# A gather ring of 72 slots instead of 64, its last eight in the memory of two buffers of the x pass, and expert units spread by another estimate of room

## The chip, the cores and the metric

One core of one Trainium2 chip. The metric is the device time of one execution in microseconds (us). Before the change three runs gave 2422.8, 2426.01 and 2431.03 us, so the median is 2426.01 us.

## The reference

The input is x (12500 nodes x 256), 200000 edges (src, dst, weight; sorted by dst) and the weights of two layers.

```python
x = x + gnn(layernorm(x))      # support = xn @ W (256x256); out[dst] += weight * support[src]; out + b
x = x + ffn(layernorm(x)[None])
# ffn: router on the mean over all nodes -> softmax over 8 experts, capacity scale, top 2, softmax of the 2
#      h = gelu(x @ W1[e] + b1[e]) (256 -> 512); y = h @ W2[e] + b2[e] (512 -> 256)
#      out = layer_norm(sum of 2 gated experts + x) * gamma + beta
```

dst is floor(12500 * u^2) with u uniform, so low nodes have many edges and high nodes few. Everything is float32.

## The kernel before

**Slots and tiles.** The edges, taken from the highest dst down, are cut into NE = 1564 slots of 128 edges. The nodes are 98 tiles of 128, numbered in the same order: tile 0 has about 5 slots, tiles 1 to 40 some 8 to 10, tile 72 about 16, tile 96 about 66 and tile 97, the last, about 158. For each slot GpSimd (POOL) issues one indirect DMA that gathers the 128 source rows into a slot of the ring G (L559). VectorE (DVE) builds a one-hot matrix with the edge weights (L1053), in a ring of 8. TensorE (PE) multiplies one by the other and accumulates in PSUM (L1374, two matmuls a slot).

**The ring.** G has RING = 64 slots. From slot 64 on, POOL waits at L552 until PE has done all slots up to three behind the one whose memory it takes (s_main at least s - 61). The first 96 slots (FRESH) gather from x itself, later ones from xr_d, a copy of x scaled by each row's 1/std. That copy is made in the x pass at the start: SyncE (SP) loads 25 groups of four tiles into XBUF = 18 buffers XS (L370), DVE takes the moments, ScalarE (ACT) scales (L773), SP stores to xr_d (L419). The groups are stored in lots of 4, 4, 4, 5, 4, 2 and 2. Groups 18 to 24 go into buffers 0 to 6 again. XS lies in the memory that the expert units use later.

**The sections.** Where PE has finished a tile's slots there is an END event: PE runs `chores` for the tiles before (transpose, product with W, transpose of the normalised row: L1321, L1325, L1326, L1330) and `begin` for the shared slots of the next tile (L1336, L1337), and ACT runs `section`, which copies PSUM to SBUF and normalises. For each group of four tiles ACT computes the roots together (`root`, L672 to L686), in the section of a tile whose number leaves 3 when divided by 4. The next section's L1330, in the tile whose number divides by 4, waits for the row XH that ACT can only make behind these roots (L692).

**The units.** All eight experts are computed ahead of the router for eight groups of tiles: 64 expert units. Up (L1346) and down (L1357) of a unit run between slots; ACT does the gelu (L753) and the copy out (L761). The first eight units have two tiles, the others four. `events()` places the units: from tile 14 on a tile has a `room`, 0.75 of its slots less 3.5, and the units are dealt out in proportion. A table of 168 due slots and kinds, EVT, goes to the chip, and PE, ACT and SP walk it in the same order. So a unit's place in the sequence of slots is fixed; only its time is not.

**PE's loop.** PE's slots run in a loop of 195 iterations of 8 slots and 4 more (L1409). The place in the ring is computed from registers at the head of each iteration: `(i & 7) * 2048`. Behind every second slot PE's sequencer compares the next due slot with its own (L1382), and where it is reached, `event` runs (L1383 and on).

**The second stage.** After slot 1563 come the router and the two chosen experts for the remaining 17 groups.

Of the kernel before, what the change touches and what calls it, by code (L numbers as in the profile page):

```python
# [4 lines left out]
P = 128  # L5
# [4 lines left out]
NE = (EDGES + 2 * P - 1) // (2 * P) * 2  # L10
FULL = EDGES // P
NC = (NE + P - 1) // P
RING, GS, OHR = 64, 16, 8
FRESH, XBUF = 96, 18
LOTS = (4, 4, 4, 5, 4, 2, 2)
SHIFT = (NT - 1) * P
LN_EPS = 1e-5
# [60 lines left out]
def events():  # L78
    share = lambda t: min(max(t, 0), NODES / P) / (NODES / P)
    slots = [NE * (share(NT - t) ** 0.5 - share(NT - 1 - t) ** 0.5) for t in range(NT)]  # L80
    most = [0.75 if t == NT - 1 else 1.0 for t in range(NT)]
    room = [max(0.0, 0.75 * slots[t] - 3.5) * most[t] if t >= 14 else 0.0 for t in range(NT)]
    size = [len(tiles(k // E)) / GT for k in range(UNITS)] + [1.0]
    free, u, out = 0.0, 0, []
    for t in range(NT):
        free += room[t] * sum(size) / sum(room)
        n = 0
        while u + n <= UNITS and (free >= size[u + n] / 2 or t == NT - 1):
            free -= size[u + n]
            n += 1  # L90
        kinds = [UPS if k == 0 else DOWNS if k == UNITS else BOTH for k in range(u, u + n)]
        mine = [(round(64 * most[t] * (k + 1) / (n + 1)) / 64, kind, u + k) for k, kind in enumerate(kinds)]
        if t == NT - 1:
            mine += [(k / 32, EXTRA, NT - 1 + k) for k in range(VIRTUAL)]
        out += [(t, *m) for m in sorted(mine)]
        if t < NT - 1:
            out.append((t, 1.0, END, t))
        u += n
    return out
# [7 lines left out]
def gnn_ffn(nc, x, dflat, srct, dstt, wt, W, b, Wr, br, W1, b1t, W2, b2, gamma, beta, cst, iota_e, evt, out):  # L107
# [13 lines left out]
    with ctx:  # L121
# [70 lines left out]
        YU = early("YU", [P, 2, GT * P])  # L192
        H = early("H", [P, 4, GT * P])
        YE = early("YE", [P, 2, GT * D])
        XS = At(w_at)("XS", [P, XBUF, GT, D])
        Gf = G[:, :, :].rearrange("p r d -> p (r d)")

        TABLES = 28
        first = At(g_at + 4 * TABLES * D)
# [2 lines left out]
        LOW = first("LOW", [P, NE], i32)  # L202
        IE, EV = first("IE", [NT, NE]), first("EV", [NT + 1, 2 * NEV])
        cmpb, cmpt = first("cmpb", [P, NC, NT], bf16), At(low_at)("cmpt", [NT, NE], bf16)
        assert first.at <= g_at + 4 * RING * D

        moments = At(yt_at)
        XST, XMV = moments("XST", [P, 2, GT, 6]), moments("XMV", [P, NT, 2])
# [152 lines left out]
        def _(e):  # L361
# [3 lines left out]
            def load_x(g):  # L365
                k = g % XBUF
                if g >= XBUF:
                    e.wait_ge(xs_st[lot_of[g - XBUF]], 16 * LOTS[lot_of[g - XBUF]])
                a, n = g * GT, len(xtiles(g)) - (g == XG - 1)
                e.dma_start(XS[:, k, 0:n, :].rearrange("p t d -> p (t d)"), x[a * P:(a + n) * P, :].rearrange("(p t) d -> p (t d)", p=P)).then_inc(xs_in[k], 16)  # L370
                if g == XG - 1:
                    e.dma_start(XS[0:LAST, k, n, :], x[(NT - 1) * P:NODES, :]).then_inc(xs_in[k], 16)

            def load_w1(u):
                if u >= 1:
# [38 lines left out]
            def store_x(b):  # L414
                for g in lots[b]:
                    k, m = g % XBUF, len(xtiles(g))
                    n = m - (g == XG - 1)
                    e.wait_ge(s_xs, g * GT + m)
                    e.dma_start(xr_d[g * GT * P:(g * GT + n) * P, :].rearrange("(p t) d -> p (t d)", p=P), XS[:, k, 0:n, :].rearrange("p t d -> p (t d)")).then_inc(xs_st[b], 16)  # L419
                    if n < m:  # L420
                        e.dma_start(xr_d[(NT - 1) * P:NODES, :], XS[0:LAST, k, n, :]).then_inc(xs_st[b], 16)

            for g in range(6):
                load_x(g)
# [109 lines left out]
        @block.gpsimd  # L534
        def _(e):
            e.wait_ge(s_flag, 2)
            r = e.alloc_register("unsorted")
            e.load([r], FLAG[0:1, 0:1])
            with e.If(e.snap(r, min_val=0, max_val=NE * P) != 0):
                flat = lambda v: v.rearrange("p n -> (p n)").rearrange("(m o) -> m o", o=1)  # L540
                with e.Fori(0, NE) as i:
                    e.wait_ge(s_c, i + 1)
                    e.sem_inc(s_step, 1)
                    for dst, src, s in zip((srct_s, dstt_s, wt_s), (sg_s, sg_d, sg_w), s_sc):
                        e.indirect_dma_start(out=flat(dst), out_offset=bass.IndirectOffsetOnAxis(ap=q_i[:, 0:1], axis=0),
                                             in_=src[:, :], in_offset=None).then_inc(s, 16)
            e.wait_ge(src_in, 32)
            for s in range(NE):
                if s >= RING:
                    e.wait_ge(s_main, s - RING + 3)  # L550
                if s >= GS:
                    e.wait_ge(gat[s % GS], 16 * (s // GS))  # L552
                if s == FRESH:
                    for l, lot in enumerate(lots):
                        e.wait_ge(xs_st[l], 16 * (len(lot) + (lot[-1] == XG - 1)))
                if s == TABLES:
                    e.wait_ge(s_tab, tab_ev)
                if rows(s):
                    e.indirect_dma_start(out=G[0:rows(s), s % RING, :], out_offset=None, in_=x if s < FRESH else xr_d,  # L559
                                         in_offset=bass.IndirectOffsetOnAxis(ap=SRC[0:rows(s), s:s + 1], axis=0)).then_inc(gat[s % GS], 16)  # L560

            e.wait_ge(s_route, 5)
            e.tensor_tensor(out=R1[:, NT - 1:NT], in0=VE[:, 0:1], in1=mhalf[:, 0:1], op=ALU.pow).then_inc(s_zr, 1)
            e.wait_ge(b1_in, 16)
            for k in range(2):
                e.wait_ge(s_route, IDX[k])
                one = e.value_load(idx_i[0:1, k:k + 1], min_val=0, max_val=E - 1)
                e.tensor_copy(b1s[:, k, :], b1a[:, bass.ds(one, 1), :].rearrange("p o f -> p (o f)")).then_inc(s_b1s, 1)

            def add_rows(n):  # L570
                g = order[n]
                m = len(tiles(g))
                e.wait_ge(s_xn, n + 1)
                if g < AHEAD:
                    e.wait_ge(s_b2, 2)
                    e.tensor_tensor(out=XN[:, n % 3, 0:m, :], in0=XN[:, n % 3, 0:m, :], in1=B2[:, :].unsqueeze(1).to_broadcast([P, m, D]), op=ALU.add).then_inc(s_xb, 1)
                e.wait_ge(gb_in, 32)
                e.tensor_tensor(out=XL[:, n % 4, 0:m, :], in0=XL[:, n % 4, 0:m, :], in1=be_bc[:, :].unsqueeze(1).to_broadcast([P, m, D]), op=ALU.add).then_inc(s_xp, 1)

            def rstd(n):  # L580
                m = len(tiles(order[n]))
                e.wait_ge(s_zv, n + 1)
                e.tensor_tensor(out=ZR[:, n % 3, 0:m], in0=ZV[:, n % 3, 0:m], in1=mhalf[:, 0:m], op=ALU.pow).then_inc(s_zr, 1)  # L583

            added = 0
            for n in range(NG):
                until = min(n + (2 if n + 1 < NG and order[n + 1] < AHEAD else 1), NG - 1)
                while added <= until:
                    add_rows(added)
                    added += 1  # L590
                rstd(n)

        @block.scalar
        def _(e):
# [173 lines left out]
            def scale_x(b):  # L768
                e.wait_ge(s_xq, 3 * b + 3)
                for g in lots[b]:  # L770
                    for j, t in enumerate(xtiles(g)):
                        r_ = LAST if t == NT - 1 else P
                        e.activation(XS[0:r_, g % XBUF, j, :], XS[0:r_, g % XBUF, j, :], ACT.Copy, scale=xr[0:r_, t:t + 1]).then_inc(s_xs, 1)  # L773

            xh_at, root_at = {}, {}
            for s in (s_as, s_at, s_pre, s_xh, s_yt):
# [124 lines left out]
        def _(e):  # L901
# [28 lines left out]
            def x_stats(g):  # L930
                b, m = g % 2, len(xtiles(g))
                e.wait_ge(xs_in[g % XBUF], 16 * (g // XBUF + 1 + (g == XG - 1)))
                if g >= 2:
                    e.wait_ge(s_xag, GT * (g - 1))
                for j in range(m):
                    r_ = x_rows(g, j)
                    e.bn_stats(XST[0:r_, b, j, :], XS[0:r_, g % XBUF, j, :]).then_inc(s_xbn, 1)
                for j in range(m):
                    r_ = x_rows(g, j)
                    e.wait_ge(s_xbn, g * GT + j + 1)  # L940
                    e.bn_aggr(XMV[0:r_, g * GT + j, :], XST[0:r_, b, j, :]).then_inc(s_xag, 1)
# [330 lines left out]
        def _(e):  # L1272
# [92 lines left out]
                with e.Else():  # L1365
                    do(u, GT)

            v_r, u_r, ev_r, due, kind, now_r, rel = (e.alloc_register(n) for n in ("section", "unit", "event", "due", "kind", "now", "ahead"))
            for r_ in (v_r, u_r, ev_r):
                e.reg_mov(r_, 0)  # L1370
            e.load([due, kind], EVT[0:1, 0:2])
# [29 lines left out]
            def slots(a, g, n):  # L1401
                for r in range(n):
# [3 lines left out]
                    if r % 2 == 1:  # L1406
                        event(a, r, g)

            with e.Fori(0, NE // OHR) as i:  # L1409
                a = e.snap(i * OHR)  # L1410
                g = e.snap((i & (RING // OHR - 1)) * (OHR * D))
                e.reg_mov(rel, e.snap(due) - a)
                slots(a, g, OHR)
            a = NE // OHR * OHR
# [138 lines left out]
```

## Time and profile before

| what | us |
|---|---|
| median of three runs | 2426.01 (2422.8 to 2431.03) |
| the profiled execution | 2431.56 |
| its span, first to last instruction | 2429.8 |
| first slot on PE | 85.25 |
| first and last gather issued on POOL | 11.29 and 1981.91 |
| last slot done on PE | 2002.2 |
| second stage, behind it | 427.3 |

Busy over the whole span: PE 2240.1 us (92%), POOL 1618.5 (67%), ACT 1184.3 (49%), DVE 1025.5 (42%). The granted clock was 0.972 of full speed on average. An engine's idle time counts only where its work is what the end waits for; the windows by stage and the timeline show that better than the shares of the whole span.

### The profile page before, as it was taken

How to read it: one execution, taken by the hardware profiler on the slowest of the kernel's cores; microseconds unless marked ns; L12 is line 12 of the kernel's file. 1: busy time of each engine (PE TensorE's matmuls, PEld its weight loads, DVE VectorE, ACT ScalarE, POOL GpSimd, SP SyncE). 2: the span in 40 equal slices, each digit the busy share in tenths (PEclk: the TensorE clock that was granted, in tenths of full speed). 3: DMA queues.
4: the chain of work that ended last, by engine and by line, in shares of the span. 5: the costliest groups of instructions: out<-in, count | busy, mean ns of one | idle time of the engine just before them, and what ended most of it. 6: DMA issues, size and time to landing. Idle time of an engine off the chain costs nothing. (4 is left out here: it accounts for less than half of the span.)

```text
span 2429.8 us, 41873 instructions
## 1 busy us (share of the span) xinstructions
PE 2240.1 (92%) x9976; PEld 1736.3 (71%) x9977; DVE 1025.5 (42%) x2959; ACT 1184.3 (49%) x3197; POOL 1618.5 (67%) x1628
## 2 busy tenths in 40 slices
PE   2488999899999999999999999999998999999997
PEld 1366777676776767777776777777776788998887
DVE  7883223222232223222322323232321246888897
ACT  3577666665665555545434343332323117556463
POOL 6677777777777777777777777777777741324241
PEclk8699999999999999999999999999999999999999
DMA  9855667666665555566556555565565533233321
GB/s 371 317 171 156 201 200 235 188 184 181 180 186 179 179 170 174 176 183 192 185 172 186 186 182 183 181 182 176 177 193 164 182 115 105 100 131 113 122 96 53
DMA packets 226708, 425.79 MB, mean 175 GB/s; under 512 B 36643, under 2 KB 134742, under 8 KB 226568
## 3 DMA queue, kind: packets, MB, share of 16 engines
q0 software_dynamic: 75008, 204.90, 28.1%
q1 hardware_dynamic: 151128, 217.12, 27.3%
q10 hardware_dynamic: 432, 2.40, 0.3%
q14 instruction: 113, 0.93, 0.1%
q8 instruction: 27, 0.44, 0.1%
HBM read 341.53 MB, written 82.75 MB: 175 GB/s over the span
## 5 line engine op out<-in xcount | busy, mean ns | idle before, releaser
L559 POOL DMA_INDIRECT G<-xr_d,SRC x1467 | 1396.7, 952 | 447.2 <-issue 295.1
L1053 DVE TENSOR_SCALAR OH<-CST,DL,WR 128x128 f32<-128x128 f32 x1564 | 563.9, 368 | 1296.7 <-PE ps L1374 1151.6
L1374 PE MATMUL ps<-G,OH 128*128 x3128 | 751.2, 394 | 92.5 <-DVE OH L1053 53.0
L1374 PEld LDWEIGHTS ps<-G,OH 128*128 128x128 f32 x3128 | 599.6, 196 | 257.2 <-issue 179.6
L1346 PE MATMUL ps<-YU,W1u 128*128 128x512 f32 (+1 forms) x1024 | 426.3, 569 | 8.5 <-ACT H L753 7.3
L1357 PE MATMUL ps<-W2u,H 128*128 128x256 f32 x1920 | 428.6, 381 | 4.9 <-issue 4.4
L1357 PEld LDWEIGHTS ps<-W2u,H 128*128 128x128 f32 x1920 | 361.4, 190 | 66.9 <-issue 19.4
L1346 PEld LDWEIGHTS ps<-YU,W1u 128*128 128x128 f32 x1024 | 195.0, 191 | 205.0 <-issue 184.9
L761 ACT ACTIVATE YE<-ps 128x512 f32<-128x512 f32 (+1 forms) x128 | 72.7, 570 | 462.7 <-PE ps L1357 462.7
L753 ACT ACTIVATE H<-ps,b1a 128x512 f32<-128x512 f32 (+1 forms) x256 | 168.6, 661 | 225.9 <-PE ps L1346 225.7
L638 ACT ACTIVATE OHX<-OHT,WR 128x128 f32<-128x128 f32 x194 | 67.2, 394 | 231.7 <-PE ps L1374 231.7
L583 POOL TENSOR_TENSOR ZR<-ZV,mhalf 128x4 f32<-128x4 f32 (+1 forms) x25 | 33.4, 1335 | 191.2 <-DVE ZV L1225 191.2
L1494 PE MATMUL ps<-W2h,Hlo 128*128 128x256 f32 x544 | 154.2, 283 | 0.0
L1494 PE MATMUL ps<-W2l,Hhi 128*128 128x256 f32 x544 | 154.1, 283 | 0.0
L1494 PE MATMUL ps<-W2h,Hhi 128*128 128x256 f32 x544 | 153.6, 282 | 0.0
L1194 DVE TENSOR_TENSOR Hlo<-Ht,Hhi 128x512 fp32r<-128x512 f32 x136 | 127.3, 950 | 59.5 <-ACT Hhi L881 59.3
L878 ACT ACTIVATE Ht<-ps,b1s 128x512 f32<-128x512 f32 x136 | 93.7, 689 | 100.0 <-PE ps L1473 100.0
L559 POOL DMA_INDIRECT G<-in_x,SRC x96 | 93.0, 969 | 45.4 <-issue 24.4
L1494 PEld LDWEIGHTS ps<-W2h,Hhi 128*128 128x128 f32 x544 | 104.3, 192 | 5.6
L1494 PEld LDWEIGHTS ps<-W2l,Hhi 128*128 128x128 f32 x544 | 104.2, 192 | 5.1
L1325 PE MATMUL ps<-Wsb,AT 128*128 128x256 f32 x412 | 106.9, 382 | 0.0
L1494 PEld LDWEIGHTS ps<-W2h,Hlo 128*128 128x128 f32 x544 | 104.1, 191 | 0.0
(206 smaller groups left out, 2330.4 us busy)
## 6 DMA issues: line engine op xcount, KB each, us to landing
W1u<-in_W SPq DMA_DIRECT2D x64, 512.0 KB
W2u<-in_W SPq DMA_DIRECT2D x64, 512.0 KB, 4.7
y_d<-YE SPq DMA_DIRECT2D x56, 512.0 KB, 5.4
G<-xr_d,SRC POOLq DMA_INDIRECT x1467, 2.9
x_d<-X SPq DMA_DIRECT2D x98, 128.0 KB, 2.1
yt_d<-YT SPq DMA_DIRECT2D x98, 128.0 KB, 2.5
XR<-in_x SPq DMA_DIRECT2D x97, 128.0 KB, 3.1
XS<-in_x SPq DMA_DIRECT2D x24, 512.0 KB, 19.3
```

What stands on the lines that cost most here:

```text
L559: e.indirect_dma_start(out=G[0:rows(s), s % RING, :], out_offset=None, in_=x if s < FRESH else xr_d, in_offset=bass.IndirectOffsetOnAxis(a ...
L638: e.activation(OHX[:, k, :], OHT[:, 1, k, :], ACT.Copy, scale=WR[:, bass.ds(odd + k, 1)]).then_inc(s_ohx, 1)
L753: e.activation(H[:, i, 0:w], ps[:, UP[i % 2], 0:w], ACT.Gelu, bias=b1a[:, u % E, i:i + 1]).then_inc(s_gelu, 1)
L761: e.activation(YE[:, u % 2, p * w:(p + 1) * w], ps[:, DN[p], 0:w], ACT.Copy).then_inc(s_ye, 1)
L878: e.activation(Ht[:, i % HB, 0:w], ps[:, 4 + i % HB, 0:w], ACT.Gelu, bias=b1s[:, i // 4, i % 4:i % 4 + 1]).then_inc(s_ht, 1)
L1053: e.tensor_scalar(OH[:, s % OHR, :], iota, DL[:, s:s + 1], WR[:, s + 1:s + 2], ALU.is_equal, ALU.mult).then_inc(s_oh, 1)
L1194: e.tensor_tensor(out=Hlo[:, h, 0:w], in0=Ht[:, i % HB, 0:w], in1=Hhi[:, h, 0:w].bitcast(f32), op=ALU.subtract).then_inc(s_hlo, 1)
L1325: e.matmul(ps[:, XB, 0:D], AT[:, c * P:(c + 1) * P], Wsb[:, c, :], start=False, stop=True, skip_group_check=True)
L1346: ins = e.matmul(ps[:, UP[i % 2], 0:m * P], W1u[:, c, i * P:(i + 1) * P], YU[:, c, 0:m * P], start=(c == 0), stop=(c == 1))
L1357: ins = e.matmul(ps[:, DN[p], h * D:(h + 1) * D], H[:, i, j * P:(j + 1) * P], W2u[:, i, :], start=(h == 0 and i == 0), stop=(i == 3), skip ...
L1374: e.matmul(ps[:, 0, 0:D], OH[:, r, :], Gf[:, bass.ds(g + r * D, D)], start=False, stop=True, skip_group_check=True).then_inc(s_main, 1)
L1494: ins = e.matmul(acc, hp[:, h, rows], wp[:, x_, f, :], start=(i == 0 and q % 2 == 0 and a == 0), stop=False, skip_group_check=True)
```

## The change

RING goes from 64 to 72. The tile G grows by 8 KB in each partition, and XS gets 16 buffers instead of 18 of its own. The two numbered 8 and 9 (INNER) are now slots 64 to 71 of G. These two buffers hold groups 8 and 9, which belong to the third lot. Before POOL gathers slot 64 it waits until that lot is stored (`s == held`). POOL's wait for PE now comes from slot 72 on, for s_main at least s - 69. Nine slots of 8 don't fit a mask, so the place in the ring is now computed as i - (i * 57 >> 9) * 9, times 2048, moved to a register and taken from there. The room of a tile is 0.8 of its slots less 3.0.

The number of units, of events (168) and of slots is the same. The units lie otherwise: at most tiles one more unit has been started than before, at a few two more or none. Tile 97 has 6 events with units instead of 7. By tile, before and after: tiles 14 to 21 had a unit each in 15, 17, 19 and 21, and have one each in 14, 16, 18, 20 and 21; tile 24 had one and has none, tile 28 had one and has none, tile 32 had none and has one, tile 68 had none and has one, tile 72 had one and has none; tiles 36, 44, 52, 56, 60 and 64 have none and tiles 40, 48 and 76 have one in both.

```diff
@@ -10,8 +10,9 @@
 NE = (EDGES + 2 * P - 1) // (2 * P) * 2
 FULL = EDGES // P
 NC = (NE + P - 1) // P
-RING, GS, OHR = 64, 16, 8
+RING, GS, OHR = 72, 16, 8
 FRESH, XBUF = 96, 18
+INNER = (8, 9)
 LOTS = (4, 4, 4, 5, 4, 2, 2)
 SHIFT = (NT - 1) * P
 LN_EPS = 1e-5
@@ -79,7 +80,7 @@
     share = lambda t: min(max(t, 0), NODES / P) / (NODES / P)
     slots = [NE * (share(NT - t) ** 0.5 - share(NT - 1 - t) ** 0.5) for t in range(NT)]
     most = [0.75 if t == NT - 1 else 1.0 for t in range(NT)]
-    room = [max(0.0, 0.75 * slots[t] - 3.5) * most[t] if t >= 14 else 0.0 for t in range(NT)]
+    room = [max(0.0, 0.8 * slots[t] - 3.0) * most[t] if t >= 14 else 0.0 for t in range(NT)]
     size = [len(tiles(k // E)) / GT for k in range(UNITS)] + [1.0]
     free, u, out = 0.0, 0, []
     for t in range(NT):
@@ -192,8 +193,17 @@
         YU = early("YU", [P, 2, GT * P])
         H = early("H", [P, 4, GT * P])
         YE = early("YE", [P, 2, GT * D])
-        XS = At(w_at)("XS", [P, XBUF, GT, D])
+        XSw = At(w_at)("XS", [P, XBUF - len(INNER), GT, D])
         Gf = G[:, :, :].rearrange("p r d -> p (r d)")
+        held = RING - GT * len(INNER)
+
+        def XS(g):
+            k = g % XBUF
+            if k in INNER:
+                a = held + INNER.index(k) * GT
+                return G[:, a:a + GT, :]
+            return XSw[:, k - sum(i < k for i in INNER), :, :]
+
 
         TABLES = 28
         first = At(g_at + 4 * TABLES * D)
@@ -202,7 +212,8 @@
         LOW = first("LOW", [P, NE], i32)
         IE, EV = first("IE", [NT, NE]), first("EV", [NT + 1, 2 * NEV])
         cmpb, cmpt = first("cmpb", [P, NC, NT], bf16), At(low_at)("cmpt", [NT, NE], bf16)
-        assert first.at <= g_at + 4 * RING * D
+        assert first.at <= g_at + 4 * (RING - GT * len(INNER)) * D
+        assert XBUF + min(INNER) >= XG
 
         moments = At(yt_at)
         XST, XMV = moments("XST", [P, 2, GT, 6]), moments("XMV", [P, NT, 2])
@@ -367,9 +378,9 @@
-                e.dma_start(XS[:, k, 0:n, :].rearrange("p t d -> p (t d)"), x[a * P:(a + n) * P, :].rearrange("(p t) d -> p (t d)", p=P)).then_inc(xs_in[k], 16)
+                e.dma_start(XS(g)[:, 0:n, :].rearrange("p t d -> p (t d)"), x[a * P:(a + n) * P, :].rearrange("(p t) d -> p (t d)", p=P)).then_inc(xs_in[k], 16)
...
@@ -550,6 +561,9 @@
                     e.wait_ge(s_main, s - RING + 3)
                 if s >= GS:
                     e.wait_ge(gat[s % GS], 16 * (s // GS))
+                if s == held:
+                    for l in sorted({lot_of[k] for k in INNER}):
+                        e.wait_ge(xs_st[l], 16 * LOTS[l])
                 if s == FRESH:
                     for l, lot in enumerate(lots):
                         e.wait_ge(xs_st[l], 16 * (len(lot) + (lot[-1] == XG - 1)))
@@ -1365,7 +1379,7 @@
                 with e.Else():
                     do(u, GT)
 
-            v_r, u_r, ev_r, due, kind, now_r, rel = (e.alloc_register(n) for n in ("section", "unit", "event", "due", "kind", "now", "ahead"))
+            v_r, u_r, ev_r, due, kind, now_r, rel, lap_r = (e.alloc_register(n) for n in ("section", "unit", "event", "due", "kind", "now", "ahead", "lap"))
             for r_ in (v_r, u_r, ev_r):
                 e.reg_mov(r_, 0)
             e.load([due, kind], EVT[0:1, 0:2])
@@ -1406,9 +1420,12 @@
                     if r % 2 == 1:
                         event(a, r, g)
 
+            LAPS, LAPS_MUL = RING // OHR, -(-512 // (RING // OHR))
+            assert all(i * LAPS_MUL >> 9 == i // LAPS for i in range(NE // OHR))
             with e.Fori(0, NE // OHR) as i:
                 a = e.snap(i * OHR)
-                g = e.snap((i & (RING // OHR - 1)) * (OHR * D))
+                e.reg_mov(lap_r, (i - (i * LAPS_MUL >> 9) * LAPS) * (OHR * D))
+                g = e.snap(lap_r, min_val=0, max_val=(LAPS - 1) * OHR * D)
                 e.reg_mov(rel, e.snap(due) - a)
                 slots(a, g, OHR)
             a = NE // OHR * OHR
```

## Rows read from the trace of the kernel before

**Rows 1.** The page, part 1: busy us (share), instructions of each engine.

```profile
PE 2240.1 (92%) x9976; PEld 1736.3 (71%) x9977; DVE 1025.5 (42%) x2959; ACT 1184.3 (49%) x3197; POOL 1618.5 (67%) x1628
```

**Rows 2.** Windows by stage: length, busy (count) of each engine, PEclk, DMA share, GB/s.

```profile
200.00:1000.00 800.00, 745.18 (x3071) 563.34 (x3070) 227.84 (x626) 475.00 (x1487) 605.83 (x638) 0.97 0.61 186
1000.00:1820.00 820.00, 809.92 (x3236) 596.59 (x3235) 239.91 (x668) 311.61 (x824) 621.21 (x653) 1.00 0.59 183
...
2002.50:2429.80 427.30, 403.00 (x2521) 361.74 (x2521) 348.32 (x757) 240.71 (x422) 128.63 (x61) 0.98 0.31 103
```

**Rows 3.** Timeline of PE, the last slots: start, us, instructions, idle before.

```profile
1964.92 7.07 PE L1374 MATMUL ps<-G,OH 128*128 x32
1971.83 7.07 PE L1357 MATMUL ps<-W2u,H 128*128 128x256 f32 x32
1978.73 23.47 PE L1374 MATMUL ps<-G,OH 128*128 x108
```

**Rows 4.** Timeline of POOL, first stretch.

```profile
11.29 1.19 POOL L559 DMA_INDIRECT G<-in_x,SRC  x1 [10.85 <-ACTq L610]
...
93.39 0.95 POOL L559 DMA_INDIRECT G<-in_x,SRC  x1 [0.30 <-issue]
...
100.35 0.95 POOL L559 DMA_INDIRECT G<-in_x,SRC  x1 [2.25 <-PE ps L1374]
...
106.53 1.00 POOL L559 DMA_INDIRECT G<-in_x,SRC  x1 [3.98 <-PE ps L1374]
```

**Rows 5.** Timeline of POOL, the last gather.

```profile
1981.91 0.91 POOL L559 DMA_INDIRECT G<-xr_d,SRC  x1 [0.30 <-PE ps L1374]
```

**Rows 6.** Waits of POOL: total us, times, longest.

```profile
POOL G L559 <- issue: 319.5, 1048, 0.3
...
POOL G L559 <- PE ps L1374: 150.4, 475, 4.0
```

**Rows 7.** Line L1330 on PE, 150 to 1000 us.

```profile
  ACT XH L692: 21.3, 12
```

**Rows 8.** Timeline of PE, tile 32.

```profile
427.70 0.54 PE L1330 MATMUL ps<-CST,XH 128*128 128x128 f32 x2 [2.13 <-ACT XH L692]
428.85 1.22 PE L1336 MATMUL ps<-G,OHX 128*128 x2 [0.61 <-ACT AS L640]
```

**Rows 9.** Timeline of PE, tile 68.

```profile
957.46 0.44 PE L1330 MATMUL ps<-CST,XH 128*128 128x128 f32 x2 [1.18 <-ACT XH L692]
```

**Rows 10.** Windows behind such waits: PEclk is the third last number.

```profile
232.00:242.00 10.00, 9.71 (x36) 7.86 (x36) 1.54 (x4) 5.70 (x19) 7.59 (x8) 0.83 0.57 155
...
427.00:437.00 10.00, 8.68 (x26) 6.88 (x27) 3.27 (x9) 5.74 (x22) 7.56 (x9) 0.66 0.77 248
...
960.00:970.00 10.00, 9.47 (x37) 8.10 (x38) 2.94 (x8) 3.24 (x12) 7.56 (x9) 0.83 0.50 145
```

**Rows 11.** Timeline of PE, tile 24.

```profile
329.78 0.79 PE L1346 MATMUL ps<-YU,W1u 128*128 128x256 f32 x1 [3.01 <-ACT H L753]
```

**Rows 12.** Line L1409, PE sequencer: ns min/median/max.

```profile
L1409 PEldq FUSED_REGOPS  x195: 147/152/176, 43.1 to 1995.7; - x195
...
L1409 PEldq COMPARE_BRANCH  x195: 76/208/219, 104.3 to 1998.8; - x195
```

**Rows 13.** Lines L1350 and L1341, the same.

```profile
L1350 PEldq FUSED_REGOPS  x64: 42/42/47, 235.2 to 1971.3; - x64
...
L1341 PEldq FUSED_REGOPS  x64: 88/88/88, 212.8 to 1955.7; - x64
```

**Rows 14.** Timeline of PE around heads of iterations.

```profile
544.84 5.61 PE L1374 MATMUL ps<-G,OH 128*128 x24
...
553.49 2.85 PE L1374 MATMUL ps<-G,OH 128*128 x12 [0.75 <-issue]
```

**Rows 15.** Timeline of SP, the third and later lots.

```profile
72.27 23.23 SPq L419 DMA_DIRECT2D xr_d<-XS  x17
```

**Rows 16.** Tile xr_d, 72 to 76.2 us.

```profile
DMA to landing us min/median/max: 7.8/9.2/14.1
```

More of the change, by code:

```diff
@@ L369, in load_x @@
                 a, n = g * GT, len(xtiles(g)) - (g == XG - 1)
-                e.dma_start(XS[:, k, 0:n, :].rearrange("p t d -> p (t d)"), x[a * P:(a + n) * P, :].rearrange("(p t) d -> p (t d)", p=P)).then_inc(xs_in[k], 16)
+                e.dma_start(XS(g)[:, 0:n, :].rearrange("p t d -> p (t d)"), x[a * P:(a + n) * P, :].rearrange("(p t) d -> p (t d)", p=P)).then_inc(xs_in[k], 16)
                 if g == XG - 1:
-                    e.dma_start(XS[0:LAST, k, n, :], x[(NT - 1) * P:NODES, :]).then_inc(xs_in[k], 16)
+                    e.dma_start(XS(g)[0:LAST, n, :], x[(NT - 1) * P:NODES, :]).then_inc(xs_in[k], 16)
             def load_w1(u):
@@ L418, in store_x @@
                     e.wait_ge(s_xs, g * GT + m)
-                    e.dma_start(xr_d[g * GT * P:(g * GT + n) * P, :].rearrange("(p t) d -> p (t d)", p=P), XS[:, k, 0:n, :].rearrange("p t d -> p (t d)")).then_inc(xs_st[b], 16)
+                    e.dma_start(xr_d[g * GT * P:(g * GT + n) * P, :].rearrange("(p t) d -> p (t d)", p=P), XS(g)[:, 0:n, :].rearrange("p t d -> p (t d)")).then_inc(xs_st[b], 16)
                     if n < m:
-                        e.dma_start(xr_d[(NT - 1) * P:NODES, :], XS[0:LAST, k, n, :]).then_inc(xs_st[b], 16)
+                        e.dma_start(xr_d[(NT - 1) * P:NODES, :], XS(g)[0:LAST, n, :]).then_inc(xs_st[b], 16)
             for g in range(6):
@@ L772, in scale_x @@
                         r_ = LAST if t == NT - 1 else P
-                        e.activation(XS[0:r_, g % XBUF, j, :], XS[0:r_, g % XBUF, j, :], ACT.Copy, scale=xr[0:r_, t:t + 1]).then_inc(s_xs, 1)
+                        e.activation(XS(g)[0:r_, j, :], XS(g)[0:r_, j, :], ACT.Copy, scale=xr[0:r_, t:t + 1]).then_inc(s_xs, 1)
             xh_at, root_at = {}, {}
@@ L936, in x_stats @@
                     r_ = x_rows(g, j)
-                    e.bn_stats(XST[0:r_, b, j, :], XS[0:r_, g % XBUF, j, :]).then_inc(s_xbn, 1)
+                    e.bn_stats(XST[0:r_, b, j, :], XS(g)[0:r_, j, :]).then_inc(s_xbn, 1)
                 for j in range(m):
```

## The prediction

> **What bounds the kernel now.** I read the shares of the whole span first [rows 1]: PE 92% busy, POOL 67%. Such a mean can hide a stage, so the windows by stage come next [rows 2]. From 200 to 1000 us PE is busy for 745 of 800 us, from 1000 to 1820 for 810 of 820; POOL has the same share, 76%, in both. That 76% is not slack: in POOL's timeline every gather takes 0.95 us and 0.30 us passes before the next [rows 4, 5], so POOL runs at one gather in 1.254 us from 11.29 us to the end. The waits of POOL say the same: 1048 gaps for issue with a longest of 0.3 us, and of the 475 put down to PE only two are longer, 2.25 and 3.98 us [rows 4, 6]. The other waits "for PE" are thus no full ring; they are the same 0.30 us under another name.
>
> So two chains run side by side, and the end of the slots tells which is last [rows 3, 5]. POOL issues its last gather at 1981.91 us. PE at 1978.73 us still has 108 matmuls, 54 slots, and does them without a gap until 2002.2 us. Data for them had long been there. PE is last by about 19.5 us, and the second stage (427.3 us [rows 2]) follows. I counted how many gathers POOL is ahead when PE finishes each slot (L559 against L1374 in the timelines): never under 18, so PE never waits for a gather; at most 61 in the first slots, where the ring is full and the two long waits lie, and 55 later, near slot 1494. A time is saved or lost here only if PE's sum of work and stalls from 85 to 2002 us changes, or if POOL becomes later by more than 19.5 us.
>
> **Ring of 72.** It removes POOL's two waits: 2.25 - 0.30 + 3.98 - 0.30 = 5.6 us [rows 4]. With eight more slots, slot 72 needs PE's first three slots at about 103 us, and PE has them by 90. POOL then ends 5.6 us earlier, but it is not last: 0 us. The ring is full nowhere later, before or after. One unit of four tiles more ahead of a slot is 7.07 us down [rows 3] and as much up, 14 us, or 11 gathers; with the 4 or 5 that POOL gains at the start the 48 slots ahead between 400 and 1000 us become about 63. That would fill 64 slots (limit 61) and does not fill 72 (limit 69). So the ring is what makes the other schedule free for POOL. The bound above is that all the later slots stall POOL: it has 19.5 us to lose first, so 0 again.
>
> **Slots 64 to 71 in XS's memory.** The new wait stands in POOL's queue ahead of all later gathers. POOL comes to slot 64 at 93.39 us [rows 4]. The third lot's four stores are issued from 72.27 to 76.03 us [rows 15] and land 7.8 to 14.1 us later [rows 16], the last at about 90.1 us. The cover is 3 us. If it is gone, say by 5 us, POOL starts the rest 2 us late and still ends before PE: 0. No load or store moves in SP's queue; SP's stores of the units' results shift with the units and are not waited for closely.
>
> **The units' places.** What changes on PE is which stalls are covered. Between 150 and 1000 us PE waits 12 times for XH, 21.3 us in all [rows 7]. They lie in tiles 8, 12, 16, 20, 32, 36, 44, 52, 56, 60, 64 and 68: tiles divisible by 4 without a unit. The ones with a four-tile unit (40, 48, 72, 76) have none, since 14 us of PE work cover ACT's roots. Each wait has a tail: 0.6 to 0.7 us for AS [rows 8], and a stretch at 1.2 GHz instead of 2.4 GHz right behind it. In a window of 10 us the mean granted clock falls to 0.83, which loses 1.7 us, and once to 0.66, 3.4 us [rows 10]. From 1000 us on the clock is full. By tiles:
> - Tile 32 gets a unit: -(2.13 + 0.61 + 3.4) = -6.1 us [rows 8, 10].
> - Tile 68 gets one: -(1.18 + 0.7 + 1.7) = -3.6 us [rows 9, 10].
> - Tile 72 loses one. It has 16 slots; the wait shrinks from 2.1 us (tile 52) to 1.2 (tile 68) as tiles grow, so I take 0.7 + 0.7 + 1.7 = +3.1 us.
> - Tiles 24 and 28 lose a small unit. Small units don't cover: there PE waited 3.01 and 2.14 us for the gelu, since ACT was busy with the roots [rows 11], and lost clock too. Now the XH wait stands in its place: about -1.7 and +1.0.
> - Tiles 16 and 20 get small units, the reverse: about -0.5 each.
>
> Together -8.3, rounded to -8 us; bounds 0 (every covered wait turns up at another tile) and -14 (16, 20, 24 and 28 all come free, some 1.5 us each). Later tiles have no such waits, apart from the 3.84 us one in tile 97, whose surroundings stay.
>
> **The head of the loop.** This is the part that costs. At the head of each of 195 iterations PE's sequencer works for itself: 0.208 us of branch and 0.152 us of register steps [rows 12]. The latter holds four steps (i * 8, the mask, times 2048, due less a), so 38 ns a step; two steps take 42 and three with a shift 88 ns [rows 13], 21 to 29 ns each. The new head has three more arithmetic steps (times 57, shift, times 9, less, for one mask) and one move: 4 x 38 = 0.15 us, and if they don't fit one instruction another start of about 0.06 us; I take 0.18. The least is 3 x 29 = 0.09, the most 5 x 46 + 0.06 = 0.29.
>
> Is it seen? Matmuls start every 0.216 us, so x24 should last 0.379 + 23 x 0.216 = 5.35 us; a stretch behind a section takes 5.61, and where the event falls right before the head PE idles for 0.75 us [rows 14]. The last 108 matmuls show nothing of it: 0.379 + 107 x 0.216 = 23.5, as measured [rows 3]. So the head is hidden where the sequencer has a lead, and seen where an event has eaten it. I compared, for all 195 heads, the start of the first matmul with that of its last register step: in some 70 it follows at once (0.10 us), in the others it has between 0.04 and 1.9 us of lead. Adding 0.18 us to each and taking off the lead gives 14 us; 0.09 gives 6, 0.29 gives 24. Some 1 us is absorbed by waits for XH and the one-hots.
>
> The Trainium skill, TensorE: Matmul & The Clock Gate, in its first table, gives TensorE an engine queue 64 deep. By that rule the sequencer could be so far ahead that a few register steps would never be seen, and this term would be 0. The idle time for "issue" in [rows 14] does not agree: at those heads nothing was queued.
>
> **Sum.** 2431.6 (the profiled execution) + 0 - 8 + 14 - 1 = 2436.6. That execution lies 5.5 us above the median of the three runs, so 2431 us as a median, 5 us or 0.2% more.
>
> **Rivals.**
> 1. The head costs little: the steps are computed while PE still has matmuls queued, which the last 108 matmuls speak for and the 0.75 us gaps against. Then the stalls' gain is all that is left, at most 14 less 6 of the least head: 2426 - 8 = 2418 us. Faster.
> 2. The head costs all that its bound allows: several instructions for the place, and the leads are shorter than counted, because units and sections now fall elsewhere. +24, and only -4 from the stalls: 2426 + 20 = 2446 us. Slower. It decides from 0.2 us of extra steps on. For it: a separate move exists for every compare. Against: the steps fuse well elsewhere [rows 13].
> 3. ACT in the small tiles becomes the bound: two small units more before tile 21 put gelus into sections that come every 10 us. The gelu waits of 3.01 us [rows 11] with their clock loss of up to 3.4 could appear at 16, 18 and 20 beside the XH waits: +10 on the sum, 2439 us. For it: ACT is busiest there. Against: units in tiles 15, 17, 19 and 21 had under 1 us of it.
> 4. The change does nothing on PE that can be seen, since POOL alone gains. That is the case of 2426 us and lies inside the forecast's range.
>
> **How the numbers follow.** A run of this kernel can't tell less than 0.3%, 7.3 us, from no change. Forecast with rival 4: 0.45, its own range 2424 to 2438. Rival 1: 0.22. Rival 2: 0.22. Rival 3: 0.11. The range takes in most of rivals 1 and 2: 2417 to 2445 us. Faster by more than 7.3 us is rival 1: 0.22. Slower is rival 2, half of 3 and the upper edge of the forecast: 0.34. The same: 0.44.
>
> **What would show it.** POOL's timeline without the waits of 2.25 and 3.98 us and its last gather at about 1976 us; no gap longer than 0.3 us at slot 64. No XH wait in tiles 32 and 68, one in 24, 28 and 72; the XH total near 20 us. The register steps of the loop's head at about 0.33 us instead of 0.152, and PE's idle time for issue ahead of L1374 up from 34 us by several us. PE's last slot at about 2007 us, with POOL further ahead of it than before. I am wrong if the last slot is before 2000 us, or if PE ends within 5 us of the last gather, which would make POOL the bound.

## The result, and the profile after

The changed kernel takes 2435.43 us (median of 12 runs, 2429.98 to 2439.07), the kernel before 2428.58 us (12 runs, 2422.8 to 2431.38). The ratio is 1.0032, 95% interval 1.002 to 1.0044: 6.85 us slower by the medians. The interval doesn't reach 1, so the kernel is slower, though by less than the 7.3 us that the prediction took as the least to tell. The forecast was 5 us more, 2431 us from a median of 2426.01. The profiled execution has a span of 2436.3 us, against 2429.8.

Part 1 of the page and the windows by stage of the changed kernel (columns as in [rows 1, 2]):

```profile
PE 2240.5 (92%) x9976; PEld 1731.8 (71%) x9977; DVE 1025.6 (42%) x2959; ACT 1183.5 (49%) x3197; POOL 1613.1 (66%) x1628
...
200.00:1000.00 800.00, 744.49 (x3067) 558.67 (x3065) 225.13 (x620) 473.43 (x1479) 601.98 (x636) 0.98 0.62 187
1000.00:1820.00 820.00, 803.53 (x3200) 590.48 (x3201) 238.22 (x662) 309.58 (x825) 620.79 (x655) 1.00 0.60 182
...
2010.00:2436.30 426.30, 402.73 (x2521) 362.08 (x2521) 348.31 (x757) 241.03 (x422) 128.50 (x61) 0.98 0.31 103
```

The work is the same: 2240.5 us of PE against 2240.1, and the second stage lasts 426.3 us, against 427.3. So the time was lost between matmuls, before the last slot. Between 1000 and 1820 us PE is busy for 803.5 us instead of 809.9 at the same full clock, with 3200 matmuls instead of 3236; between 200 and 1000 us it does four fewer at a slightly better clock. These windows don't hold the same slots, because the units lie elsewhere, so they don't place the loss. Experiment 3, with the units where they were, places it.

The ends of the two chains, PE's timeline first, then POOL's (start, us, instructions, idle before), which answer to [rows 3 to 5]:

```profile
1970.86 7.93 PE L1388 MATMUL ps<-G,OH 128*128 x36
1978.63 7.07 PE L1371 MATMUL ps<-W2u,H 128*128 128x256 f32 x32
1985.54 24.34 PE L1388 MATMUL ps<-G,OH 128*128 x112
```

```profile
93.24 0.95 POOL L573 DMA_INDIRECT G<-in_x,SRC  x1 [0.30 <-issue]
...
951.89 1.00 POOL L573 DMA_INDIRECT G<-xr_d,SRC  x1 [4.85 <-PE ps L1388]
...
1975.24 0.90 POOL L573 DMA_INDIRECT G<-xr_d,SRC  x1 [0.30 <-PE ps L1388]
```

PE's last slot ends at 2009.9 us, 7.7 us later; POOL's last gather starts at 1975.2 us, 6.7 us earlier. The two waits of [rows 4] are gone and slot 64 (93.24 us) has no wait for the stores. But one new wait for a full ring, 4.85 us, stands at slot 746. Counted as for the prediction, POOL's lead over PE after slot 100 lies between 35 and 69 slots; 69 is the limit. Before it lay between 18 and 55.

The waits for ACT: line L1344 on PE from 150 to 1000 us; then PE's timeline at a gelu wait in tile 16, in tile 24 and in tile 32. They answer to [rows 7, 8, 11].

```profile
  ACT XH L706: 15.9, 10
```

```profile
234.59 1.99 PE L1360 MATMUL ps<-YU,W1u 128*128 128x256 f32 x8 [2.67 <-ACT H L767]
...
333.78 0.44 PE L1344 MATMUL ps<-CST,XH 128*128 128x128 f32 x2 [2.85 <-ACT XH L706]
...
441.45 0.38 PE L1344 MATMUL ps<-CST,XH 128*128 128x128 f32 x2
```

The head of the loop: the instructions of L1425 and L1428 in PE's sequencer (ns min/median/max), which answer to [rows 12], and PE around heads, which answers to [rows 14].

```profile
L1425 PEldq FUSED_REGOPS  x195: 208/212/238, 43.1 to 2003.3; - x195
L1428 PEldq FUSED_REGOPS  x195: 152/157/157, 43.4 to 2003.6; - x195
L1425 PEldq COMPARE_BRANCH  x195: 76/208/215, 103.2 to 2006.5; - x195
```

```profile
556.39 5.81 PE L1388 MATMUL ps<-G,OH 128*128 x24
565.37 2.85 PE L1388 MATMUL ps<-G,OH 128*128 x12 [0.89 <-issue]
```

Two fused instructions, 212 and 157 ns, stand where one of 152 ns and a single step of 36 ns stood. From the start of the first of them to the start of the step that sets the first matmul's address, the median was 0.307 us and is now 0.485: 0.178 us more. The same stretch of 24 matmuls lasts 5.81 us instead of 5.61, and the gap where an event falls right before the head 0.89 us instead of 0.75.

### The profile page after: what moved, and what is told of

Its sections match the earlier page's. It is cut to its first block and busy times, and to the rows that moved or that the text cites. A ratio compares the mean times of both kernels' runs of the same rounds, so it can differ in the third digit from the quotient of the medians.

```text
span 2436.3 us, 41866 instructions
## 1 busy us (share of the span) xinstructions
PE 2240.5 (92%) x9976; PEld 1731.8 (71%) x9977; DVE 1025.6 (42%) x2959; ACT 1183.5 (49%) x3197; POOL 1613.1 (66%) x1628
```

## The experiments

Each was timed in five rounds beside the kernel before; ratios are to that kernel on the same chip. "Ends" are the start of POOL's last gather and the end of PE's last slot.

**1. The ring alone** (the changed kernel with the old estimate of room):

```diff
-    room = [max(0.0, 0.8 * slots[t] - 3.0) * most[t] ...
+    room = [max(0.0, 0.75 * slots[t] - 3.5) * most[t] ...
```

> The changed kernel with the old estimate of room (0.75 of the slots less 3.5): ring of 72, shared buffers and the new loop head alone, units where they were. Theory (the head of the loop costs 14 us, the moved units give back 7 to 8): about 14 us over the kernel before, ratio 1.006, with the 12 waits of PE for XH where they were (21 us). Rival (the head is hidden and the moved units cost): ratio 1.000. Rival (the wait ahead of slot 64 or the memory shared with it costs): POOL has a gap at slot 64 or ends later than 1982 us.

Measured: 2441.55 us against 2429.63, ratio 1.0048 [1.0036, 1.006], +11.9 us. Ends 1973.0 and 2011.5 us. The larger ring, with the head that it needs, makes the kernel slower, although POOL's last gather comes 8.9 us earlier. POOL has no gap at slot 64. The 12 waits for XH are there as expected, but shorter, 18.4 us instead of 21.3:

```profile
  ACT XH L706: 18.4, 12
```

**2. The units' places alone** (the kernel before with the new estimate, the ring at 64 and the mask in the head):

```diff
-    room = [max(0.0, 0.75 * slots[t] - 3.5) * most[t] ...
+    room = [max(0.0, 0.8 * slots[t] - 3.0) * most[t] ...
```

> The kernel before with the new estimate of room alone: ring of 64, mask at the loop's head. Theory: the covered stalls alone show, 7 to 8 us under the kernel before, ratio 0.997, last slot on PE at about 1995 us; POOL now finds the ring full in places and ends later than 1982 us, but is not last. Rival (the ring of 72 is needed, since POOL's waits reach the end): ratio 1.000 or more, with PE waiting for gathers. Rival (the moved units cost): ratio 1.003 or more.

Measured: 2421.63 us, ratio 0.9965 [0.9953, 0.9976], -8.0 us. The ends are 1977.1 and 1987.6 us, and POOL waits for no full ring after slot 70: its lead is at most 56 slots. So the ring is not what makes the schedule possible. The waits of L1330 for ACT, 150 to 1000 us:

```profile
  ACT XH L692: 16.4, 10
```

The row is near that of the changed kernel (15.9, 10), which is to be compared with 18.4 in experiment 1: the schedule takes off 4.9 us with the ring of 64 and 2.5 us with that of 72. The two parts sum to +11.9 - 8.0 = +3.9 us against +6.85 together, within what these intervals leave open.

**3. The head alone** (ring of 64, old schedule, the place in the ring by the arithmetic of the changed kernel):

```diff
-                g = e.snap((i & (RING // OHR - 1)) * (OHR * D))
+                e.reg_mov(lap_r, (i - (i * 64 >> 9) * 8) * (OHR * D))
+                g = e.snap(lap_r, min_val=0, max_val=(RING // OHR - 1) * OHR * D)
...
```

> The kernel before with the changed kernel's register steps at the loop's head, with 64 and 8 as constants, so that the ring of 64 and the units stay as they were. Theory: this alone costs 12 to 14 us, ratio 1.0055, with the head's steps 0.18 us longer and PE's idle time ahead of the slots' matmuls up. Rival (the sequencer is far enough ahead): ratio 1.000.

**4. The same steps twice**, the second on the result of the first:

```diff
+                e.reg_mov(lap2_r, i - (i * 64 >> 9) * 8)
+                q = e.snap(lap2_r, min_val=0, max_val=7)
+                e.reg_mov(lap_r, (q - (q * 64 >> 9) * 8) * (OHR * D))
...
```

> As the one before, with the shift and products done twice in a chain (the second time on a value that it doesn't change). Theory: the lead of the sequencer is a stock that each added step eats, so doubling gives more than double: with 0.36 to 0.4 us added to each head 30 to 35 us, ratio 1.013. Rival (a fixed price a head): twice the run before. Rival (hidden): 1.000.

Measured: 2444.76 us, ratio 1.0057 [1.0045, 1.0069], +15.1 us, for the steps once; 2466.81 us, ratio 1.0151 [1.0137, 1.0165], +37.2 us, for the steps twice. The head's fused instructions, of the kernel with the steps once, then twice:

```profile
L1409 PEldq FUSED_REGOPS  x195: 208/212/238, 43.5 to 2009.1; - x195
L1412 PEldq FUSED_REGOPS  x195: 152/157/157, 43.8 to 2009.4; - x195
```

```profile
L1409 PEldq FUSED_REGOPS  x195: 201/208/236, 43.2 to 2026.3; - x195
L1413 PEldq FUSED_REGOPS  x195: 208/217/218, 43.5 to 2026.6; - x195
L1415 PEldq FUSED_REGOPS  x195: 132/132/138, 43.8 to 2026.8; - x195
```

The head is the whole of the ring's price. Nothing else differs in experiment 3, and it costs 15.1 us, about as much as ring and head together cost in experiment 1 (11.9 us, whose larger ring has the same head). The profiled executions show it growing along the loop, as a price of each head would: with the units where they were, PE is behind the kernel before by 6.4 us at slot 750, 9.4 at slot 1000, 12.9 at slot 1400 and 13.5 at the last.

The steps written twice cost 2.5 times as much, but they also take 2.4 times as long: from the first fused instruction to the first matmul's step the median is 0.732 us, so 0.425 us more than before the change, against 0.178. For each us added to a head that is 88 us against 85, so by the device times a flat price of each added us fits too. What speaks for a lead that is used up first is in the traces. I add up, over the heads from the second on, the time beyond 0.216 us between the starts of an iteration's first matmul and the matmul before it. This is 44.8 us in the kernel before, 59.0 in experiment 3 and 87.8 in experiment 4, so +14.2 and +43.0, three times as much. The device time of experiment 4 doesn't show the difference, and it ran 30.7 us at the low level of the clock between 150 and 1990 us, where the kernel before ran 61.4. So how the price grows with the steps is not settled.

In experiment 3 PE becomes late enough to fill the ring of 64: POOL waits 5.01, 2.50 and 2.40 us at slots 1496, 1526 and 1556. These lie off the critical path: the last gather starts at 1987.0 us and PE's last slot ends at 2015.7.

**5. More covered tiles.** Experiment 2 left waits in tiles divisible by 4 without a unit, beside a unit one tile off. Six units are moved there:

```diff
+MOVES = ((35, 36), (43, 44), (53, 52), (55, 56), (59, 60), (63, 64))
...
+    for a, b in MOVES:
...
+        counts[a], counts[b] = 0, 1
...
```

> The kernel before with the new estimate of room and six units moved by one tile each: 35 to 36, 43 to 44, 53 to 52, 55 to 56, 59 to 60 and 63 to 64, so that every tile divisible by 4 from 32 on has a unit. Theory (a unit in such a tile covers ACT's roots): the waits for XH in these six tiles, 9 us, with 4 us for AS and the clock behind them, are gone, 20 us of PE's sum; but POOL's last gather, at 1977 us in the run with the new room alone, then is the floor, so PE's last slot comes at 1981 to 1984 us and the time is 4 to 7 us under that run, ratio 0.994 to the kernel before. Rival (POOL is no bound): 20 us under that run, ratio 0.988. Rival (the wait moves to another tile): no change against that run, 0.9965.

Measured: 2413.22 us against 2428.98, ratio 0.9934 [0.9921, 0.9947], -15.8 us, so 7.8 us more than experiment 2 gained, where 4 to 7 were expected. PE's last slot ends at 1982.2 us. The XH waits, then PE's last slots and POOL's last gather, where PE now runs into POOL:

```profile
  ACT XH L701: 7.2, 4
```

```profile
1971.54 1.99 PE L1383 MATMUL ps<-G,OH 128*128 x8 [1.55 <-DVE OH L1062]
1976.41 3.28 PE L1383 MATMUL ps<-G,OH 128*128 x8 [2.87 <-DVE OH L1062]
...
1976.91 0.90 POOL L568 DMA_INDIRECT G<-xr_d,SRC  x1 [0.30 <-issue]
```

PE waits for one-hots four slots at a time, and DVE makes each only once its gather has landed.

**6. Fewer heads** (the schedule of experiment 2, 16 slots in an iteration, so half the heads):

```diff
-            with e.Fori(0, NE // OHR) as i:
...
+            IT = 16
+            with e.Fori(0, NE // IT) as i:
...
-                slots(a, g, OHR)
...
+                slots(a, g, IT)
...
```

> The new estimate of room with ring of 64 and the mask, and 16 slots in an iteration of PE's loop instead of 8, so 97 heads instead of 195. Theory (a head costs where the sequencer has no lead): some 10 us of PE's sum are saved against the run with the new room alone, of which POOL's floor leaves 4 to 7; ratio 0.994. Rival (twice the code in the loop costs as much in fetching as it saves): 0.9965 or more.

**7 and 8. The same with a ring of 72 and 24 slots in an iteration**, on the changed kernel, and with the six moves too:

```diff
-            with e.Fori(0, NE // OHR) as i:
...
+            IT = 24
...
+            with e.Fori(0, NE // IT) as i:
...
```

> The changed kernel with 24 slots in an iteration, the longer register steps kept, so 65 heads instead of 195. Theory: the steps' 14 us shrink to a third and the old part of the heads too, so PE's sum falls by some 20 us against the changed kernel, and POOL's last gather is 5 us earlier than with 64 slots: ratio 0.992 to 0.995 to the kernel before. Rival (the ring of 72 or its memory costs by itself): 1.000 or more.

> The one before with the six units moved. Theory: PE's sum would be 40 us under the changed kernel's, so POOL is the bound: PE's last slot within 6 us of the last gather, at 1976 to 1980 us, ratio 0.990 to 0.992. Rival (PE stays the bound): 0.987 or less. Rival (larger loop and moved units cost): 0.995 or more.

Measured: 4529.93 us (ratio 1.8644 [1.8618, 1.867]), 4318.3 us (1.7781 [1.7755, 1.7807]) and 4310.98 us (1.773 [1.7696, 1.7765]). All three expectations failed by far. Experiment 6's rival names what happened, the fetching of a larger body, but priced it at about what the fewer heads save. Three views of experiment 6: the DMA queue of instructions (packets, MB, share), PE's wait for issue (total us, times, longest), and PE's timeline:

```profile
q8 instruction: 995, 16.30, 1.6%
```

```profile
PE ps L1374 <- issue: 1234.7, 515, 9.1
```

```profile
1013.39 2.07 PE L1374 MATMUL ps<-G,OH 128*128 x4 [7.61 <-issue]
1016.13 2.07 PE L1374 MATMUL ps<-G,OH 128*128 x4 [0.67 <-issue]
```

In the changed kernel the queue carries 27 packets and 0.44 MB:

```profile
q8 instruction: 27, 0.44, 0.1%
```

The added packets are 968 in 97 iterations, 10 in each, of 16.4 KB. So the longer body is fetched anew in every iteration, and PE waits for it; experiment 7 (931 packets, 65 iterations, 14 in each) agrees. A body of 8 slots, an estimated 5 or 6 such packets by the same measure, stays. The Trainium skill, Advanced Engine Details and Errata, section ISA Cache, gives lines of 16 KB and 128 KB for TensorE. By these two figures TensorE would hold 8 lines, which is an estimate: a body of 5 or 6 fits and one of 10 does not. The packets' size and both outcomes agree with that, though the limit itself was not measured. The same section also says "Only 2 cache lines!", and with that, if it were meant for TensorE too, the body of 8 slots that stays does not agree.

**9 and 10. The six moves on the changed kernel, and the changed kernel again.** The short diff of the first is that of experiment 5.

> The changed kernel (ring of 72, longer loop head of 8 slots) with the six units moved by one tile. Theory: the parts add up on PE as long as POOL is not last. With the ring of 64 and the six moves PE came to slot 1440 with 36 gathers ahead instead of 49, so 16 us of its sum were gone, and POOL's last gather at 1977 us cut that to 5. Here the head gives back 12 to 15 us and the last gather is at 1971 to 1975 us, so PE is just last again: last slot at 1984 to 1989 us, ratio 0.994 to 0.996, no better than the ring of 64 with the same moves. Rival (the ring of 72 pays now that POOL is nearly the bound): last slot at 1976 to 1980 us, ratio 0.991 to 0.9925. Rival (the gain of the moves is lost beside the longer head): 1.000 or more.

> The changed kernel once more, on the same chip and in the same rounds as the run beside it. Theory: ratio 1.002 to 1.004, so that the sum of its two parts, 1.0048 and 0.9965, holds within the intervals. Rival (the parts hinder each other, by 3 us or more): 1.0045 or more.

Measured: 3238.84 us (ratio 0.9975 [0.9949, 1.0002]) and 3227.32 us (0.9939 [0.9913, 0.9965]). These ran on another chip, where the kernel before took 3245.03 us too. The changed kernel is there 0.6% faster than the kernel before, against an expectation of 1.002 to 1.004. In the trace of experiment 10 the queue of instructions has its 27 packets, yet POOL waits for PE's slots, on a ring that is full all the time (total us, times, longest):

```profile
POOL G L573 <- PE ps L1388: 736.2, 310, 13.0
```

PE's timeline there has gaps for issue of up to several us between matmuls that are otherwise of the usual length. The first fused instruction of the head takes 212 ns at the median as elsewhere, but up to 1396 ns, and the mean granted clock is 0.887 instead of 0.985. What held the sequencer back on that chip was not found. These two don't say which part of the change does what, but they show that its sign isn't the same on every chip.

**11 and 12. The six moves with the ring of 72, and with the ring of 64, side by side** on one chip:

> The changed kernel with the six units moved by one tile, once more, since in the run before all kernels, the one before the change too, took 3240 us on that chip. As then: the head gives back 12 to 15 us of PE's 16, POOL's last gather is at 1971 to 1975 us, PE's last slot at 1984 to 1989 us, ratio 0.994 to 0.996. Rival (the ring of 72 pays now that POOL is nearly the bound): 0.991 to 0.9925.

> The ring of 64 with the new room and the six moves, in the same rounds as the one beside it. Theory: ratio 0.9934 as before, PE's last slot within 6 us of POOL's last gather, and 1 to 4 us under the ring of 72. Rival: the ring of 72 is the faster by 2 us or more.

Measured: 2413.54 us (0.9939 [0.9925, 0.9952]) and 2412.33 us (0.9932 [0.9919, 0.9946]), the kernel before at 2428.72. The last slots on PE, of experiment 11 and then of experiment 12, and DVE ahead of them in 12:

```profile
1961.11 24.34 PE L1397 MATMUL ps<-G,OH 128*128 x112
```

```profile
1967.11 2.90 PE L1383 MATMUL ps<-G,OH 128*128 x8 [2.86 <-DVE OH L1062]
1972.22 3.78 PE L1383 MATMUL ps<-G,OH 128*128 x8 [2.21 <-DVE OH L1062]
1977.11 6.08 PE L1383 MATMUL ps<-G,OH 128*128 x16 [1.11 <-DVE OH L1062]
```

```profile
1975.41 0.34 DVE L1062 TENSOR_SCALAR OH<-CST,DL,WR 128x128 f32<-128x128 f32 x1 [0.89 <-DMA G<-xr_d,SRC]
```

With 72 slots POOL ends early (last gather 1971.5 us) and PE, slowed by its head, is last at 1985.4. With 64 slots PE is faster but meets the gathers, which end at 1977.7, and finishes at 1983.2. The difference, 1.2 us, is not resolved, and 1 to 4 us were expected. The plain version is as fast as any that was run: ring of 64, the mask, the new estimate and the six moves, 16.4 us (0.7%) under the kernel before.

## Why the prediction was right, and where not

- **PE bounds, POOL's gain is worth nothing.** Right. Experiment 1 moved the last gather 8.9 us forward and the kernel became slower.
- **Ring of 72: 5.6 us off POOL, last gather near 1976.** Right, 1975.2 us.
- **"The ring is full nowhere later", a lead of about 63.** Wrong. The lead reaches the limit of 69, and POOL waits 4.85 us at slot 746. The term of the lead was mis-sized: I held PE's pace fixed, but the new head makes PE late by the very microseconds of the next term. It cost nothing, as POOL's last gather starts 34 us before PE's last slot ends. Also wrong: the conclusion that 64 slots would be filled and that the ring makes the schedule free. With the schedule alone the lead is 56 and no wait follows (experiment 2).
- **Slots 64 to 71 in XS's memory: 0.** Right; 0.30 us ahead of slot 64, as everywhere.
- **The units' places: -8 us.** Right, -8.0 in experiment 2, though less so tile by tile. Tiles 32 and 68 lost their waits, and 24 and 28 got them (2.85 and 2.21 us), as said. Tile 72 got none, only 0.65 us for AS; it was priced at +3.1. Tiles 16 and 20 lost their XH waits but got gelu waits of 2.67 and 1.88 us: rival 3's mechanism, at two tiles. The XH total is 15.9 us, where I wrote near 20. In experiment 2, XH, AS and gelu waits shrank by 4.9, 0.7 and 0.9 us between 150 us and the last slot. The rest of the forecast, the clock's share, is not shown. The time at the low level (1.2 GHz) between 150 and 1990 us is 61.4 us before and 41.0 in experiment 2, but also 47.8 in experiment 1 and 30.7 in experiment 4, whose units lie as before. One profiled execution of each can't assign it. As tile 72's +3.1 was too much and 16 and 20 came out otherwise, the hit to the tenth of a us is partly luck.
- **The head: +0.18 us, +14 us.** Right in size and mechanism. In the trace, counted as for experiments 3 and 4, the heads that come right behind a slot's matmul cost 14.8 us before (47 of them) and 24.1 after (67), the others 30.0 and 36.6: +15.9 us. Experiment 3, which has only this, measured +15.1 us of device time. The prediction's way of counting, once more with the measured 0.178 us, gives 15 us, and 40 us with the 0.425 us of experiment 4, which measured 37.2. The 1 us taken off for absorption is not seen.
- **Rivals.** Rival 1 (the head is hidden) fell with experiments 3 and 4. Rival 2 (the head costs its full bound, 2446 us) was too large: 15.1 us, not 24. Rival 3 came at two tiles (16 and 20) and not with its 10 us. The total is the sum of the parts, 15.1 - 8.0 = 7.1 us against 6.85. PE's last slot ends at 2009.9 us instead of the predicted 2007.

The groups of PE's slots in the kernel before, in experiment 3 and in the changed kernel (line engine op, count | busy, mean ns | idle before it, by releaser):

```profile
L1374 PE MATMUL ps<-G,OH 128*128 x3128 | 751.2, 394 | 92.5 <-DVE OH L1053 53.0 <-issue 34.3
L1374 PE MATMUL ps<-G,OH 128*128 x3128 | 754.2, 394 | 102.3 <-DVE OH L1053 58.0 <-issue 38.5
L1388 PE MATMUL ps<-G,OH 128*128 x3128 | 752.8, 393 | 104.7 <-DVE OH L1067 63.2 <-issue 35.5
```

I expected the head's price under "issue". Experiment 3 differs from the kernel before in the head alone, and only 4.2 us of it stand there; 5.0 us are put down to the one-hots and 3.0 us are in the busy time of the slots. The last part is there because a gap of 0.2 us within a pipelined stretch hardly shows as idle: the stretch of 24 matmuls simply lasts 5.81 us instead of 5.61. The busy time also moves with the clock, so it is a rough measure. Who looks for such a cost must read the length of a stretch of equal matmuls, as in [rows 14].

## What to carry to other kernels

A few register steps at the head of a hot loop are work of the bounding engine where its sequencer (the part that computes addresses and issues) is not ahead of it: here 0.18 us at 195 heads cost 15 us, so a ring whose size is a power of two, with a mask, beat a larger ring with a division. Before a buffer is made larger, count how far the producer is ahead of the consumer at each step; here the larger ring gave time only to an engine that was not last. And test a change of several parts by its parts: one part gained 8 us, the other lost 12 to 15.

## What the runs showed of the hardware that I had not expected

- A loop body of 16 or 24 slots instead of 8 made the kernel 1.8 times slower: its instructions came by DMA again in each iteration (995 packets instead of 27), and TensorE's mean granted clock was 0.74, with 1235 us of waits for issue.
- Under half of the added register steps shows in the time: +0.178 us at 195 heads are 34.7 us, and cost 15.1 (experiment 3); +0.425 us are 83 us, and cost 37.2 (experiment 4).
- The indirect gather kept a pace of 1.25 us (0.95 and 0.30 between) wherever it didn't wait, in experiments 1 to 5, 11 and 12. With PE faster, it becomes the floor: with the ring of 64 the last gather started at 1976.9 to 1977.7 us in experiments 2, 5 and 12.
- One chip ran the kernel before in 3245 us instead of 2429, and the changed kernel there in 3227.
